# A recommender tower with cross layers: half of the products fused into the sum on VectorE, and one chunk of the first layer split into fp32r passes

## The chip, the cores and the metric

The kernel runs on one core of a Trainium2 chip. The core's engines work side by side, each through its own queue of instructions in order, and wait for one another by semaphores: TensorE (PE) multiplies matrices into PSUM, VectorE (DVE) and ScalarE (ACT) read PSUM and SBUF, GpSimd (POOL) reads SBUF alone, and SyncE (SP) issues DMAs. The metric is the device time of one execution in microseconds (us), lower is better.

## The reference, cut to what matters

512 examples, 32 fields, 32 dimensions. Layer 0 takes products of all pairs of fields and mixes them to 128 maps; layer 1 takes products of the 32 fields with those 128 maps and mixes them again to 128 maps. A small dense tower follows.

```python
e = stack([tbl_f[ids[:, f]] for f in range(32)], axis=1)    # (512, 32, 32)
prev, outs = e, []
for W in (filter_0, filter_1):                              # (32*32, 128), (32*128, 128)
    z = einsum('bhd,bmd->bhmd', e, prev).reshape(b, h * m, d)
    prev = relu(einsum('bpd,pn->bnd', z, W))
    outs.append(prev)
h = concat([sum(concat(outs, axis=1), axis=-1), dense_ctx], axis=1)
y = relu(relu(h @ W_top1 + b_top1) @ W_top2 + b_top2) @ W_top3
```

## The kernel before

The pairs (example, dimension) are the columns. 128 of them make a tile, four tiles a group, and there are 32 groups. The first two groups and the last ones are written out, the ones between run in a hardware loop of three groups a turn (`over_groups`, L97 and on).

**Layer 1, for a tile `u` of a group `g`.** The sum over fields is turned round: for every field h, TensorE multiplies layer 0's output by the field's filter, and the result is scaled by the field's value and then summed over the 32 fields. Four fields fill one PSUM bank (128 columns of a tile on the partitions, 4 x 128 maps along the bank), so a tile has NK = 8 banks, and each bank is made by three matmuls of fp32r operands (high x high, L895; high x low, L896; low x high, L903). Six banks of PSUM are used in a ring: bank k can be written when bank k-6 has been scaled (`layer1`, waits on `act_scaled` and `dve_scaled`). `y_ready` counts finished banks.

**Scaling and summing.** The value of a field is a number per partition (`es`). ScalarE scales banks 0, 1, 3, 5, 6 of each tile, one instruction for each field (L559, 128x128), VectorE the banks 2, 4, 7, one instruction for a bank (L724, 128x512, `es` broadcast). Both write `prod`, which holds all 32 fields of a tile, two fields interleaved word by word (`[F // 2, N, 2]`); the filters of VectorE's banks are stored in that interleaved order (`filters_by_bank`), so it writes without a step, while ScalarE writes every second word. `prod` has three buffers. GpSimd then adds the first 6 fields onto the next 6 (`fold`, L436), and VectorE sums the 26 fields that are left, in two halves of 64 maps each (`reduce`, L737).

**Layer 0, for the next group.** It has KP = 5 chunks of 128 pairs. GpSimd multiplies the pairs of fields of chunk k (L426, `z`), ScalarE rounds them to fp32r (L520, `z_hi`), GpSimd takes the rest (L416, `z_lo`), and TensorE makes three fp32r matmuls of a chunk (L876 to L878), one of the last chunk (L874). `WHOLE = 1` says that chunk 0 is not split: TensorE multiplies it in fp32 (L868). The matmuls of layer 0 for group g+1 stand between the banks of group g, at the places (tile, bank) in `Z_USED_AT`; the tables `Z_AT`, `Z_LO_AT` and `Z_HI_AT` say where GpSimd and ScalarE do theirs. VectorE also takes the rest of layer 0's output (L704), sums it (L710), transposes the fields' values (L679) and sums layer 1's output (L743, L748, L754), once a group each.

The order on each engine is written out by hand in its `body`: a loop over tiles and banks, with the other work hung at given places. On VectorE the halves of a tile's sum stand at bank 6 of the next tile and bank 2 of the one after.

## Time and profile before

| what | value |
|---|---|
| timed runs (three) | 843.12 to 845.85 us, median 843.94 us |
| profiled execution, first to last instruction | 841.7 us |
| TensorE busy | 834.0 us, 99% of the span |
| VectorE busy | 803.9 us, 96% |
| ScalarE busy | 782.8 us, 93% |
| GpSimd busy | 726.7 us, 86% |
| TensorE's granted clock | 1.000 of full speed |

The profiled execution has no time of its own beside the span of its instructions, 841.7 us; the median of the timed runs is 2.2 us above it. Busy time counts each moment once, however many instructions overlap in it. L12 is line 12 of the kernel.

### The profile page before, as it was taken

To read this page: it belongs to the slowest core of one execution; us is meant where nothing else is said; L and a number is where in the kernel's file an instruction comes from. 1 tells how busy PE (TensorE), PEld (TensorE's weight loads), DVE (VectorE), ACT (ScalarE), POOL (GpSimd) and SP (SyncE) were. 2 spreads that over 40 slices of the span, in tenths; PEclk is the share of its full clock that TensorE was granted. 3 is DMA by queue.
4 is the path that set the end of the run, shared out by engine and by line. 5 is a ranking of instruction groups with operands and counts; after the bars stand their busy time and mean duration, and the time that the engine had idled before them with its cause. 6 is when DMAs were issued, how large, how long until landed. Compare 5 with 4: busy or idle time off the path is not lost.

```text
span 841.7 us, 17220 instructions
## 1 busy us (share of the span) xinstructions
PE 834.0 (99%) x3595; PEld 670.1 (80%) x3595; DVE 803.9 (96%) x877; ACT 782.8 (93%) x2779; POOL 726.7 (86%) x550
## 2 busy tenths in 40 slices
PE   8999999999999999999999999999999999999998
PEld 6688888888888888888888888888888888888777
DVE  7699999999999999999999999999999999999996
ACT  4799999999999999999999999999999999999984
POOL 5899888999888899888899888899988799988871
PEclk9999999999999999999999999999999999999999
DMA  5541132332132232122232122332123223212000
GB/s 154 181 134 50 46 85 79 82 85 62 32 84 78 83 84 72 33 73 78 83 84 81 34 62 80 82 83 84 44 50 84 78 84 84 51 44 76 1 13 1
DMA packets 62101, 60.17 MB, mean 71 GB/s; under 512 B 26203, under 2 KB 37083, under 8 KB 62078
## 3 DMA queue, kind: packets, MB, share of 16 engines
q1 hardware_dynamic: 57982, 57.80, 23.3%
q0 software_dynamic: 4096, 2.11, 2.9%
q8 instruction: 9, 0.15, 0.1%
q14 instruction: 14, 0.11, 0.1%
HBM read 55.51 MB, written 4.31 MB: 71 GB/s over the span
## 4 chain that ended last, share of the span: by engine, by line
PE 94%; DVE 2%; DMA 1%; POOL 1%; issue 1%; SPq 0%; ACT 0%; DVEq 0%
PE ps_y L895 27%; PE ps_y L903 27%; PE ps_y L896 27%; PE ps_c L868 3%; PE ps_c L878 3%; PE ps_c L877 2%; PE ps_c L876 2%; POOL gat L447 1%; DVE csum L737 1%; PE ps_c L874 1%; DVE prod L724 1%; DMA prod<-w 0%; DMA gat<-table,rows 0%; DMA ids_and_bounds_sb<-ids_and_bounds 0%; PE ps_y L999 0%
## 5 line engine op out<-in xcount | busy, mean ns | idle before, releaser
L559 ACT ACTIVATE prod<-ps_y,es 128x128 f32<-128x128 f32 x2560 | 719.7, 490 | 37.3 <-PE ps_y L903 34.0
L737 DVE TENSOR_REDUCE csum<-prod 128x64 f32<-128x1664 f32 (+2 forms) x256 | 478.6, 1870 | 0.2
L895 PE MATMUL ps_y<-w_hi,c_both 128*128 128x512 f32 x1024 | 415.4, 406 | 1.8 <-POOL w_lo L454 1.0
L903 PE MATMUL ps_y<-w_hi,c_both 128*128 128x512 f32 x1024 | 399.6, 390 | 0.0
L896 PE MATMUL ps_y<-w_lo,c_both 128*128 128x512 f32 x1024 | 399.5, 390 | 0.0
L724 DVE TENSOR_TENSOR prod<-ps_y,es 128x512 f32<-128x512 f32 x384 | 256.0, 680 | 23.6 <-PE ps_y L903 22.4
L436 POOL TENSOR_TENSOR prod<-prod 128x768 f32<-128x768 f32 (+1 forms) x128 | 240.3, 1878 | 35.9 <-ACT prod L559 28.7
L895 PEld LDWEIGHTS ps_y<-w_hi,c_both 128*128 128x128 f32 x1024 | 192.4, 188 | 54.2 <-issue 10.4
L896 PEld LDWEIGHTS ps_y<-w_lo,c_both 128*128 128x128 f32 x1024 | 192.4, 188 | 48.2 <-issue 8.2
L903 PEld LDWEIGHTS ps_y<-w_hi,c_both 128*128 128x128 f32 x1024 | 192.2, 188 | 42.1
L426 POOL TENSOR_TENSOR z<-first,second 128x512 f32<-128x512 f32 x155 | 198.2, 1295 | 25.0 <-PE ps_c L874 24.9
L416 POOL TENSOR_TENSOR z_lo<-z,z_hi 128x512 fp32r<-128x512 f32 x121 | 154.2, 1293 | 1.3 <-issue 1.3
L407 POOL DMA_INDIRECT gat<-table,rows_now x116 | 111.6, 962 | 28.1 <-issue 21.8
L520 ACT ACTIVATE z_hi<-z 128x512 fp32r<-128x512 f32 x90 | 71.9, 799 | 0.0
L710 DVE TENSOR_REDUCE h<-c_both 128x1024 f32 (+1 forms) x32 | 38.7, 1209 | 0.0
L878 PE MATMUL ps_c<-z_lo,w_hi 128*128 128x512 f32 x90 | 36.6, 407 | 0.0
L877 PE MATMUL ps_c<-z_hi,w_lo 128*128 128x512 f32 x90 | 34.9, 388 | 0.0
L876 PE MATMUL ps_c<-z_hi,w_hi 128*128 128x512 f32 x90 | 34.9, 388 | 0.0
L868 PE MATMUL ps_c<-z,w_sum 128*128 128x512 f32 x68 | 34.7, 591 | 0.0
L520 ACT ACTIVATE z_hi<-z,copy_sb 128x512 fp32r<-128x512 f32 x31 | 27.1, 874 | 0.0
L543 ACT ACTIVATE c_parts<-csum 128x512 f32<-128x512 f32 x31 | 25.2, 812 | 0.0
L704 DVE SCALAR_TENSOR_TENSOR c_both<-ps_c,c_both 128x512 fp32r<-128x512 f32 x31 | 21.2, 683 | 0.0
(119 smaller groups left out, 290.1 us busy)
## 6 DMA issues: line engine op xcount, KB each, us to landing
second<-et_scratch SPq DMA_DIRECT2D x155, 256.0 KB, 3.8
first<-et_scratch SPq DMA_DIRECT2D x31, 256.0 KB, 3.3
et_scratch<-gat SPq DMA_DIRECT2D x62, 64.0 KB
prod<-w SPq DMA_DIRECT2D x4, 512.0 KB, 4.5
h_scratch<-h_sums SPq DMA_DIRECT2D x120, 2.0 KB
gat<-table,rows_now POOLq DMA_INDIRECT x116, 2.4
wt_sb<-wt SPq DMA_DIRECT2D x2, 512.0 KB
rows_now<-rows SPq DMA_DIRECT2D x30, 2.0 KB, 1.8
```

Of the source, the lines that this page charges most:

```text
L407: pool.indirect_dma_start(out=gat[:, g.r, u * D:(u + 1) * D], out_offset=None, in_=table, in_offset=bass.IndirectOffsetOnAxis(ap=rows_now[ ...
L416: nc.gpsimd.tensor_tensor(z_lo[:, k, :], z[:, k, :], z_hi[:, k, :].bitcast(F32), ALU.subtract).then_inc(z_lo_ready, splits_at_once(g))
L426: nc.gpsimd.tensor_tensor(z[:, k, :], first[:, :], second[:, k, :], ALU.mult).then_inc(z_ready, 1)
L436: nc.gpsimd.tensor_tensor(high, high, low, ALU.add).then_inc(folded, 1)
L520: nc.scalar.activation(z_hi[:, k, :], z[:, k, :], ACT.Copy, scale=copy_sb[:, 0:1] if k == LASTK else 1.0).then_inc(z_hi_ready, splits_at_o ...
L559: last = nc.scalar.activation(prod[:, buffer_of(g, u), h // 2, :, h % 2], ps_y[:, bank_of(g, u, k), j * N:(j + 1) * N], ACT.Copy, scale=es ...
L724: nc.vector.tensor_tensor(prod[:, buffer_of(g, u), pairs, :, :], ps_y[:, bank_of(g, u, k), :].rearrange("p (a n t) -> p a n t", n=N, t=2), ...
L737: nc.vector.tensor_reduce(csum[:, g.r, maps, u], prod[:, buffer_of(g, u), fields_folded(g, u) // 2:F // 2, maps, :].rearrange("p a n t -> ...
L878: nc.tensor.matmul(ps_c[:, :], w0_hi[:, k, :], low, start=False, stop=False)
L895: nc.tensor.matmul(out, hi, w_hi, start=True, stop=False)
L896: nc.tensor.matmul(out, hi, w_lo, start=False, stop=False)
L903: nc.tensor.matmul(out, lo, w_hi, start=False, stop=True).then_inc(y_ready, 1)
```

## The change

ScalarE now scales four banks of a tile (0, 2, 4, 6), and VectorE the other four (1, 3, 5, 7). `prod` keeps 16 fields instead of 32: VectorE no longer writes products of its own but adds them onto ScalarE's. For each field of its bank it runs one instruction, `scalar_tensor_tensor`, which multiplies the 128 columns of PSUM by the field's value (read per partition from `es`) and adds the 128 products that ScalarE has left in the partner bank's place, in the same place. So VectorE's bank k waits for ScalarE's bank k-1. GpSimd folds 4 fields onto the next 4, and VectorE's sum runs over the 12 that are left. Chunk 0 of layer 0 is split like the chunks 1 to 3: one more rounding on ScalarE, one more subtraction on GpSimd, and three fp32r matmuls in the place of the one in fp32, at (1, 0) instead of (0, 6). The raw filters get SBUF of their own instead of lying in `prod`, and a wait of ScalarE on the filters in group 0 goes.

```diff
-WHOLE = 1
+WHOLE = 0
-ACT_BANKS = ((0, 1, 3, 5, 6),) * TG
-DVE_BANKS = tuple(tuple(k for k in range(NK) if k not in a) for a in ACT_BANKS)
-FOLD = 6
-FOLD_LAST = (10, 10, 10, 8)
+ACT_BANKS = ((0, 2, 4, 6),) * TG
+PARTNER = {1: 0, 3: 2, 5: 4, 7: 6}
+DVE_BANKS = (tuple(PARTNER),) * TG
+SCALED = HB * len(ACT_BANKS[0])
+FOLD = 4
+FOLD_LAST = (6, 6, 6, 6)
...
-        prod = sb("prod", [P, BUFS, F // 2, N, 2])
+        prod = sb("prod", [P, BUFS, SCALED // 2, N, 2])
+        w1_raw = sb("w1_raw", [P, F, N])
+        w0_raw = sb("w0_raw", [P, 2 * KP, N])
...
+        def place_of(u, k):
+
+            return HB * ACT_BANKS[u].index(k)
...
-            Z_LO_AT = {1: (1, 2), 2: (3, 4)}
+            Z_LO_AT = {0: (0,), 1: (1, 2), 2: (3, 4)}
...
-                    h = HB * k + j
-                    last = nc.scalar.activation(prod[:, buffer_of(g, u), h // 2, :, h % 2],
+                    h, place = HB * k + j, place_of(u, k) + j
+                    last = nc.scalar.activation(prod[:, buffer_of(g, u), place // 2, :, place % 2],
...
-            Z_HI_AT = {(1, 1): (0, 3), (1, 2): (0, 5), (1, 3): (1, 0), (1, 4): (1, 5)}
+            Z_HI_AT = {(1, 0): (0, 1), (1, 1): (0, 3), (1, 2): (0, 5), (1, 3): (1, 0), (1, 4): (1, 5)}
...
-                fields = slice(HB * k, HB * (k + 1))
-                pairs = slice(HB // 2 * k, HB // 2 * (k + 1))
-                nc.vector.tensor_tensor(
-                    prod[:, buffer_of(g, u), pairs, :, :],
-                    ps_y[:, bank_of(g, u, k), :].rearrange("p (a n t) -> p a n t", n=N, t=2),
-                    es[:, g.r, u, fields].rearrange("p (a t) -> p a t", t=2).unsqueeze(2).to_broadcast([P, HB // 2, N, 2]),
-                    ALU.mult).then_inc(dve_scaled, 1)
+                dve.wait_ge(act_scaled, signals(ACT_BANKS, g, u, PARTNER[k]))
+                for j in range(HB):
+                    h, place = HB * k + j, place_of(u, PARTNER[k]) + j
+                    summed = prod[:, buffer_of(g, u), place // 2, :, place % 2]
+                    last = nc.vector.scalar_tensor_tensor(out=summed, in0=ps_y[:, bank_of(g, u, k), j * N:(j + 1) * N],
+                                                          scalar=es[:, g.r, u, h:h + 1], in1=summed,
+                                                          op0=ALU.mult, op1=ALU.add)
+                last.then_inc(dve_scaled, 1)
...
-            Z_USED_AT = ((0, 6), (1, 6), (2, 1), (2, 4), (2, 6))
+            Z_USED_AT = ((1, 0), (1, 6), (2, 1), (2, 4), (2, 6))
```

VectorE's queue, in the loop, from bank 2 of a group's first tile (the second half of a sum, then the next bank, the sum of layer 0's output and a first half). Before:

```order
L724 TENSOR_TENSOR prod<-ps_y,es 128x512 [waits y_ready]
L737 TENSOR_REDUCE csum<-prod 128x64
L721 REGISTER_ALU
L724 TENSOR_TENSOR prod<-ps_y,es 128x512 [waits y_ready]
L710 ISA [waits c_lo_ready]
L710 TENSOR_REDUCE h<-c_both 128x16
L733 ISA
L734 ISA [waits folded]
L735 ISA [waits act_scaled]
L737 TENSOR_REDUCE csum<-prod 128x64 [waits dve_scaled]
```

The same place after the change, from bank 1:

```order
L728 SCALAR_TENSOR_TENSOR prod<-ps_y,es,prod 128x128 [waits act_scaled]
L728 SCALAR_TENSOR_TENSOR prod<-ps_y,es,prod 128x128 x3
L740 TENSOR_REDUCE csum<-prod 128x64
L723 REGISTER_ALU
L724 REGISTER_ALU [waits y_ready]
L728 SCALAR_TENSOR_TENSOR prod<-ps_y,es,prod 128x128 [waits act_scaled]
L728 SCALAR_TENSOR_TENSOR prod<-ps_y,es,prod 128x128 x3
L713 ISA [waits c_lo_ready]
L713 TENSOR_REDUCE h<-c_both 128x16
```

Each bank of VectorE's is now four instructions of 128 columns instead of one of 512, and the first of the four waits for ScalarE as well as for TensorE.

TensorE's queue, in the loop, where chunk 0 of layer 0 stands. Before, behind bank 6 of the first tile:

```order
L903 MATMUL ps_y<-w_hi,c_both 128x512
L867 REGISTER_ALU [waits c_lo_ready]
L868 MATMUL ps_c<-z,w_sum 128x512 [waits z_ready]
L97 REGISTER_ALU
L895 MATMUL ps_y<-w_hi,c_both 128x512 [waits dve_scaled,act_scaled]
```

After, behind bank 0 of the second tile:

```order
L906 MATMUL ps_y<-w_hi,c_both 128x512
L874 REGISTER_ALU [waits c_lo_ready]
L879 MATMUL ps_c<-z_hi,w_hi 128x512 [waits z_lo_ready]
L880 MATMUL ps_c<-z_hi,w_lo 128x512
L881 MATMUL ps_c<-z_lo,w_hi 128x512
L898 MATMUL ps_y<-w_hi,c_both 128x512 [waits dve_scaled,act_scaled]
```

One fp32 matmul has become three of fp32r, and it waits for GpSimd's rest of the chunk (`z_lo`) instead of the product itself.

GpSimd's queue, in the loop, for a group's first tile. Before:

```order
L426 TENSOR_TENSOR z<-first,second 128x512 [waits z_lo_ready]
L97 REGISTER_ALU [waits pairs_in2]
L426 TENSOR_TENSOR z<-first,second 128x512 [waits z_lo_ready]
L97 REGISTER_ALU [waits pairs_in3]
L426 TENSOR_TENSOR z<-first,second 128x512 [waits z_lo_ready]
L432 ISA
L433 ISA [waits act_scaled]
L436 TENSOR_TENSOR prod<-prod 128x768 [waits dve_scaled]
```

After:

```order
L432 TENSOR_TENSOR z<-first,second 128x512 [waits z_lo_ready]
L420 REGISTER_ALU
L99 REGISTER_ALU [waits z_hi_ready]
L422 TENSOR_TENSOR z_lo<-z,z_hi 128x512 [waits l0_done]
L99 REGISTER_ALU [waits pairs_in2]
L432 TENSOR_TENSOR z<-first,second 128x512 [waits z_lo_ready]
L99 REGISTER_ALU [waits pairs_in3]
L432 TENSOR_TENSOR z<-first,second 128x512 [waits z_lo_ready]
L438 ISA
L442 TENSOR_TENSOR prod<-prod 128x512 [waits dve_scaled,act_scaled]
```

The subtraction of chunk 0 has come in behind the first product, and the fold has 512 columns instead of 768.

## Rows read from the trace of the kernel before

**Rows 1.** The page's first part: busy time, share of the span, instructions.

```profile
PE 834.0 (99%) x3595; PEld 670.1 (80%) x3595; DVE 803.9 (96%) x877; ACT 782.8 (93%) x2779; POOL 726.7 (86%) x550
```

**Rows 2.** Windows: stretch, its length, busy time (instructions) by engine, clock, DMA.

```profile
10.00:20.00 10.00, 8.21 (x38) 6.16 (x37) 7.33 (x21) 6.22 (x18) 6.12 (x7) 1.00 0.47 143
...
427.55:452.63 25.08, 25.08 (x110) 20.22 (x109) 24.57 (x27) 24.06 (x88) 22.49 (x18) 1.00 0.28 71
```

**Rows 3.** The chain that ended last, in order of time: start, us, what.

```profile
427.55 0.86 PE ps_c L868 x2
452.63 0.86 PE ps_c L868 x2
```

**Rows 4.** Waits: who waited for whom, total us, times, longest.

```profile
DVE prod L724 <- PE ps_y L903: 22.4, 34, 2.3
...
PE ps_y L895 <- DVE prod L724: 0.8, 1, 0.8
```

**Rows 5.** VectorE by line and shape: count, busy us, mean ns, idle before.

```profile
L737 DVE TENSOR_REDUCE csum<-prod 128x64 f32<-128x1664 f32 x248 | 465.5, 1877 | 0.0
...
L737 DVE TENSOR_REDUCE csum<-prod 128x64 f32<-128x1408 f32 x6 | 9.7, 1611 | 0.0
...
L838 DVE SCALAR_TENSOR_TENSOR z_lo<-ps_c,z_hi 128x480 fp32r<-128x480 f32 x4 | 2.6, 652 | 1.1 <-ACT z_hi L626 1.1
...
L845 DVE TENSOR_SCALAR second<-ps_y,bt_sb 128x480 f32<-128x480 f32 x1 | 0.7, 718 | 1.0 <-PE ps_y L1001 1.0
...
L673 DVE SCALAR_TENSOR_TENSOR w_lo<-w_hi,copy_sb,w_sum 128x128 fp32r<-128x128 f32 x1 | 0.3, 346 | 0.0
...
L698 DVE SCALAR_TENSOR_TENSOR c_both<-ps_h,c_both 128x128 fp32r<-128x128 f32 x1 | 0.3, 291 | 0.1
...
L693 DVE TENSOR_TENSOR z_lo<-z,z_hi 128x128 fp32r<-128x128 f32 x1 | 0.3, 284 | 0.0
```

**Rows 6.** VectorE's timeline in one group: start, us, line, shapes, idle before.

```profile
429.73 1.88 DVE L737 TENSOR_REDUCE csum<-prod 128x64 f32<-128x1664 f32 x1
431.52 1.28 DVE L724 TENSOR_TENSOR prod<-ps_y,es 128x512 f32<-128x512 f32 x2
432.72 1.87 DVE L737 TENSOR_REDUCE csum<-prod 128x64 f32<-128x1664 f32 x1
...
438.09 0.69 DVE L724 TENSOR_TENSOR prod<-ps_y,es 128x512 f32<-128x512 f32 x1 [0.51 <-PE ps_y L903]
```

**Rows 7.** VectorE's timeline in the first 20 us.

```profile
3.56 0.29 DVE L662 TENSOR_SCALAR rows<-neg,ids_and_bounds_sb 128x12 uint32<-128x12 f32 x1
3.76 0.21 DVE L654 CAST idf<-ids_and_bounds_sb 128x116 f32<-128x116 int32 x1
...
7.28 0.69 DVE L670 TENSOR_TENSOR w_lo<-w_sum,w_hi 128x512 fp32r<-128x512 f32 x1
7.89 0.35 DVE L673 SCALAR_TENSOR_TENSOR w_lo<-w_hi,copy_sb,w_sum 128x128 fp32r<-128x128 f32 x1
...
16.57 0.29 DVE L698 SCALAR_TENSOR_TENSOR c_both<-ps_h,c_both 128x128 fp32r<-128x128 f32 x1
16.77 0.54 DVE L684 TENSOR_TENSOR z<-c_parts,ps_y 128x384 f32<-128x384 f32 x1
```

**Rows 8.** ScalarE: L559 alone in one group's window; then L520 by form.

```profile
427.55:452.63 25.08, 22.56 (x82) 1.00 0.28 71
...
L520 ACT ACTIVATE z_hi<-z 128x512 fp32r<-128x512 f32 x90 | 71.9, 799 | 0.0
```

**Rows 9.** GpSimd by line and shape.

```profile
L436 POOL TENSOR_TENSOR prod<-prod 128x768 f32<-128x768 f32 x124 | 229.0, 1847 | 25.3 <-ACT prod L559 23.8
...
L416 POOL TENSOR_TENSOR z_lo<-z,z_hi 128x512 fp32r<-128x512 f32 x121 | 154.2, 1293 | 1.3 <-issue 1.3
```

**Rows 10.** The timeline of all engines near the end.

```profile
830.29 3.42 DVE L737 TENSOR_REDUCE csum<-prod 128x64 f32<-128x1536 f32 x2
...
833.74 0.43 ACT L548 ACTIVATE c_end<-csum 128x128 f32<-128x128 f32 x1 [0.89 <-DVE csum L737]
...
834.33 0.38 PE L1001 MATMUL ps_y<-z_lo,wt_hi 128*128 128x480 f32 x1
```

More of the change, by code:

```diff
@@ L174, in tower @@
         y_sb = sb("y_sb", [1, B])
-        w1_raw, w0_raw = (prod[:, b, :, :, :].rearrange("p a n t -> p (a n t)").rearrange("p (h n) -> p h n", n=N)
-                          for b in (2, 1))
         ids_sb = ids_and_bounds_sb[:, 0:TILES]
@@ L430, in fold @@
                 count = fields_folded(g, u)
-                last_bank = (2 * count - 1) // HB
-                pool.wait_ge(act_scaled, signals(ACT_BANKS, g, u, last_bank))
-                pool.wait_ge(dve_scaled, signals(DVE_BANKS, g, u, last_bank))
+                folded_banks = ACT_BANKS[u][:(2 * count - 1) // HB + 1]
+                pool.wait_ge(act_scaled, signals(ACT_BANKS, g, u, folded_banks[-1]))
+                pool.wait_ge(dve_scaled, signals(DVE_BANKS, g, u, max(k for k in DVE_BANKS[u] if PARTNER[k] in folded_banks)))
                 buf = buffer_of(g, u)
@@ L592, in body @@
                     for k in range(NK):
-                        if number == 0 and (u, k) == (2, 0):
-                            act.wait_ge(w1_lo_ready, NK - 2)
-                            act.wait_ge(w1_last_lo, 2)
                         if number == 0 and (u, k) == (0, 3):
@@ L719, in scale @@
                         dve.wait_ge(es_ready, g.times(1, 1))
-                    wait(dve, reduced, g.times(TG * HALVES, (u + 1 - BUFS) * HALVES))
                 dve.wait_ge(y_ready, g.times(TG * NK, u * NK + k + 1))
-                fields = slice(HB * k, HB * (k + 1))
-                pairs = slice(HB // 2 * k, HB // 2 * (k + 1))
-                nc.vector.tensor_tensor(
-                    prod[:, buffer_of(g, u), pairs, :, :],
-                    ps_y[:, bank_of(g, u, k), :].rearrange("p (a n t) -> p a n t", n=N, t=2),
-                    es[:, g.r, u, fields].rearrange("p (a t) -> p a t", t=2).unsqueeze(2).to_broadcast([P, HB // 2, N, 2]),
-                    ALU.mult).then_inc(dve_scaled, 1)
+                dve.wait_ge(act_scaled, signals(ACT_BANKS, g, u, PARTNER[k]))
[6 more added lines that the diff above has]
+                last.then_inc(dve_scaled, 1)
             def reduce(g, u, half):
@@ L736, in reduce @@
                 maps = slice(half * N // HALVES, (half + 1) * N // HALVES)
-                nc.vector.tensor_reduce(csum[:, g.r, maps, u], prod[:, buffer_of(g, u), fields_folded(g, u) // 2:F // 2, maps, :].rearrange("p a n t -> p n a t"),
+                nc.vector.tensor_reduce(csum[:, g.r, maps, u], prod[:, buffer_of(g, u), fields_folded(g, u) // 2:SCALED // 2, maps, :].rearrange("p a n t -> p n a t"),
                                         AX.XY, ALU.add).then_inc(reduced, 1)
@@ L1052, in filters_by_bank @@
 def filters_by_bank(w1):
-    w = w1.reshape(NK, HB, N, N).transpose(2, 0, 1, 3)
-    out = np.empty((N, NK, HB * N), w1.dtype)
-    for k in range(NK):
-        bank = w[:, k]
-        if k in DVE_BANKS[0]:
-            bank = bank.reshape(N, HB // 2, 2, N).transpose(0, 1, 3, 2)
-        out[:, k] = bank.reshape(N, HB * N)
-    return out.reshape(N, F, N)
+    return np.ascontiguousarray(w1.reshape(F, N, N).transpose(1, 0, 2))
 def row_picks():
```

## The prediction

> **What bounds the kernel now.** I read the page's busy times first. TensorE is busy in 99% of the span, but VectorE stands at 96% and ScalarE at 93% [rows 1], so no engine has much room, and what the change does to VectorE matters as much as what it does to TensorE. The chain of work that ended last runs through TensorE and passes the same place, layer 0's chunk 0 in fp32, once a group: from 427.55 to 452.63 us, a period of 25.08 us [rows 3]. In the window of just that group TensorE is busy 25.08 of 25.08 us, VectorE 24.57, ScalarE 24.06, GpSimd 22.49 [rows 2]. The list of waits says the same from the other side: VectorE waited 22.4 us in all for TensorE's banks, TensorE once for VectorE, 0.8 us [rows 4], and in VectorE's timeline of the group there is one gap, 0.51 us, ended by TensorE [rows 6]. So TensorE sets the period, and VectorE follows at a distance of 0.51 us in 25.08, or 2%.
>
> **VectorE's work in a group, taken apart.** Mean durations overlap, so I count from start to start. A sum over 1664 columns begins at 429.73 and the next instruction at 431.52: 1.79 us. The two products that follow begin at 431.52 and the sum after them at 432.72: 0.60 us each [rows 6]. A group has 8 half sums and 12 products: 8 x 1.79 + 12 x 0.60 = 14.32 + 7.20 = 21.52 us. The rest of the 24.57, 3.05 us, are the once-a-group instructions (L679, L704, L710, L743, L748, L754), which the change leaves as they are.
>
> **The sums get shorter.** They run over 12 fields instead of 26, 768 columns instead of 1664. From 1408 to 1664 columns the duration grows from 1611 to 1877 ns [rows 5], 1.04 ns a column, so 896 columns less are 0.93 us less: 1.79 - 0.93 = 0.86 us, 6.88 us for eight. VectorE gains 7.44 us a group.
>
> **The products get longer; this is the disputed cost.** 12 instructions of 512 columns become 64 of 128 columns, which read PSUM and SBUF, take their scalar from SBUF per partition, and write where they read. No row before has all of this. The nearest row is L698, a scalar_tensor_tensor of 128x128 out of PSUM and SBUF with a constant as its scalar: 291 ns [rows 5], and the next instruction begins 0.20 us after it, at 16.77 after 16.57 [rows 7]. That is the lower end.
>
> What does the scalar from SBUF add? L673, the same shape from SBUF with such a scalar, takes 346 ns, against 284 for L693, the same shape without one; L845 with one takes 718 ns at 480 columns out of PSUM, L838 without one 652 [rows 5]. So 62 to 66 ns in the duration. Is it also in the spacing? Two places say yes. L662, 12 columns with two such scalars, begins at 3.56 and the next at 3.76, 0.20 us for a dozen columns. And L673 began 0.61 us after L670, the usual spacing of 512 columns, and still took its full 0.35 us, so nothing of the scalar's load had been done while L670 ran [rows 7]. I take 0.20 + 0.062, rounded to 0.265 us, as that start to start is read to a hundredth. The upper end without a new effect is 0.28, half a hundredth for each reading and the larger of the two increments. 64 x 0.265 = 16.96 us, against 7.20 before.
>
> **VectorE's new group:** 6.88 + 16.96 + 3.05 = 26.89 us, over today's period. The waits that come in cost nothing beside it: VectorE's bank k waits for ScalarE's bank k-1, and ScalarE becomes the lighter engine. Once VectorE is the slowest, TensorE fills the ring of six banks ahead of it and ScalarE finishes its own banks early.
>
> **The other engines.** ScalarE has 64 instead of 80 products, each 22.56 / 80 = 0.28 us of a group [rows 8], so 4.5 us less, and one rounding more, at most 0.80 us [rows 8]: about 20.4 us. GpSimd's four folds go from 1.85 us to what 512 columns cost, 1.29 [rows 9], 2.2 us less, and one subtraction of 1.29 comes in: about 21.6 us. The fold waits for VectorE's bank 3 and must be done by VectorE's bank 5 of the next tile, some five banks later at 1.06 us each plus two sums, 7.0 us; before the longest stretch of its own GpSimd has three products and the new subtraction, 4 x 1.29 = 5.2 us, and the fold makes 6.5. It fits. TensorE: the fp32 chunk took 0.86 us [rows 3]; the other 106 matmuls of the group share 25.08 - 0.86 = 24.22, or 0.2285 us each, so three in fp32r take 0.69 and the group 24.90 us. That gain of 0.18 us a group is real, but it now ends in a wait for VectorE. TensorE's clock should not fall for having gaps: in the stretch from 10 to 20 us TensorE was busy 8.21 of 10 us at a granted clock of 1.00, the level of 2.4 GHz [rows 2].
>
> A rule of the Trainium skill (VectorE: DVE Perf Modes, The TRN2 errata) gives a VectorE instruction out of PSUM 120 cycles of 0.96 GHz beside its columns: 258 ns for 128, before the scalar. By that the estimate would be 0.32 us, 20.5 us for 64, and some 160 us more on the run. L698's spacing of 0.20 us [rows 7] speaks against it, and the sum goes by the row.
>
> **The sum.** From group 1's start to the last group's start there are 30 periods. Each goes from 25.08 to 26.89 us, +1.81, together +54 us. For the two ends I take nothing: in group 0 VectorE waits for TensorE and can take more work, and at the end VectorE's last sum (830.29 + 3.42 = 833.7, then ScalarE's 0.43 to 834.17) was no later than TensorE's own last products, which began until 834.33 [rows 10], so shorter sums win nothing there. Span 841.7 + 54 = 896 us; the timed median stood 2.2 us over the profiled span, so **898 us**.
>
> **The rivals.**
>
> *A, the scalar's load is hidden.* If VectorE fetches the next instruction's scalar while it reads PSUM, leaving one of its paths to SBUF free, the spacing is 0.20 us: 12.8 + 6.88 + 3.05 = 22.7 us, below TensorE's 24.90. Then TensorE stays the bound and the split pays: 30 groups by 0.18 us, -5 us, 839 us. This is the side opposite to my forecast, and it decides at a spacing of (24.90 - 9.93) / 64 = 0.234 us. For it speaks that neither of my two places has an instruction out of PSUM behind another one; against it, both places and L845.
>
> *C, the step of two words costs.* VectorE's old products wrote four fields without a step, and the sums read pairs of words. The new instruction reads and writes every second word of `prod`, and no row of VectorE's does that. If a word alone costs as much as a pair, 128 columns stream like 256: another 128 x 1.04 = 0.13 us, spacing 0.40, 25.5 + 9.93 = 35.4 us a group, +10.3 us by 30, **1154 us**. Against it: ScalarE writes exactly these places today, 0.28 us for 128 columns, without a visible penalty, though it is another engine. The Trainium skill (Vector Engine (DVE) Microarchitecture Reference, Measured stream behaviour on trn2) has this as a rule: full rate only for runs of two neighbouring words, and 1.73 to 1.98 ns a column where every element hops; an estimate from its figures is 0.35 to 0.39 us an instruction. The Trainium skill (SBUF — State Buffer, Door 1: The DMA port swizzle, the note on cachelines) says otherwise, that two hits in a line of 16 bytes suffice, which a step of 8 bytes gives. No run here shows which holds.
>
> *D, the waits come first.* VectorE's wait for ScalarE could leave gaps though no engine is full: where ScalarE does two pieces of layer 0 and a bank in a row (0.80 + 1.1 us) behind a bank, VectorE's partner bank comes late. Under a full VectorE such a gap is covered by its own backlog; at a spacing below 0.234 it lies beside TensorE's ring, 6 banks by 0.69 us, or 4.1 us. A small loss on rival A, giving about 844 us: no change.
>
> **How the numbers follow.** My forecast, VectorE the bound by the scalar's cost, spacing 0.245 to 0.28: 0.57. A: 0.20. C: 0.18. D and what lies between: 0.05. A measurement of this kernel can tell about 0.3% (2.5 us) from no change. Faster takes A without its neighbours, 0.20; same 0.03; slower 0.77. Within my forecast, the spacing's end of 0.28 gives 17.92 + 9.93 = 27.85 us, +83 us, 927 us; the lower end, 0.245, 25.61, +16, 860 us. A range from 860 to 927 would hold only 0.57, so it reaches to A and takes that in: 835 to 930, holding 0.80 with D; C is left out.
>
> **What would show it.** In the changed profile: the mean of L740 near 944 ns (0.86 start to start); the spacing of L728, 0.265 where I am right, 0.20 under A, 0.35 or more under C; the period between two of TensorE's chunk 0, 26.9 us; VectorE with no gap in a group, TensorE's waits at L898 ended by VectorE's L728; three matmuls of L879 to L881 taking 0.69 us. The prediction is wrong if L728's spacing is under 0.234, or if GpSimd's fold ends VectorE's waits.

## The result and the profile after

| what | before | after |
|---|---|---|
| timed runs (four each), median | 844.05 us (843.12 to 845.85) | 885.48 us (885.35 to 885.73) |
| ratio of after to before | | 1.0492, 95% interval 1.0479 to 1.0505 |
| profiled execution, first to last instruction | 841.7 us | 883.7 us |

The change makes the kernel 4.9% slower. The forecast was 898 us; 885 lies 13 us below it and inside its range.

The page of the changed kernel, busy time by engine, which answers to [rows 1]:

```profile
PE 860.6 (97%) x3625; PEld 667.9 (76%) x3625; DVE 861.5 (97%) x2541; ACT 702.2 (79%) x2297; POOL 693.3 (78%) x580
```

VectorE has 57.6 us of busy time more. ScalarE and GpSimd, relieved by the change, now stand still for a fifth of the span, and the longest wait of the kernel is ScalarE's. The list of waits (who, for whom; us in total, times, longest), beside [rows 4]:

```profile
ACT prod L565 <- PE ps_y L906: 138.6, 238, 2.6
POOL prod L442 <- DVE prod L728: 55.3, 36, 10.0
POOL prod L442 <- ACT prod L565: 50.9, 30, 1.9
...
PE ps_y L898 <- DVE prod L728: 10.9, 38, 0.5
```

TensorE waited for VectorE once before and does so 38 times now. That VectorE is the cause, and not merely full too, is seen in its own timeline of one group (start, us, line, shapes, idle time before where there is any), beside [rows 6]:

```profile
449.13 1.23 DVE L713 TENSOR_REDUCE h<-c_both 128x1024 f32 x1
...
452.15 2.17 DVE L728 SCALAR_TENSOR_TENSOR prod<-ps_y,es,prod 128x128 f32<-128x128 f32 x8
454.22 0.97 DVE L740 TENSOR_REDUCE csum<-prod 128x64 f32<-128x768 f32 x1
455.08 2.18 DVE L728 SCALAR_TENSOR_TENSOR prod<-ps_y,es,prod 128x128 f32<-128x128 f32 x8
...
472.78 1.13 DVE L728 SCALAR_TENSOR_TENSOR prod<-ps_y,es,prod 128x128 f32<-128x128 f32 x4 [0.16 <-issue]
...
475.72 1.21 DVE L713 TENSOR_REDUCE h<-c_both 128x1024 f32 x1
```

Read it from start to start. Eight fused products begin at 452.15 and the sum behind them at 454.22: 2.07 / 8 = 0.258 us each. The sum begins at 454.22 and the next product at 455.08: 0.86 us. The only idle time that the timeline lists in 26.59 us is 0.16 us, and no engine ended it. The window of that group, in the columns of [rows 2], says the same:

```profile
449.13:475.72 26.59, 26.15 (x112) 20.37 (x111) 26.43 (x79) 20.96 (x70) 20.93 (x19) 1.00 0.25 69
```

VectorE is busy 26.43 of 26.59 us. (TensorE's 26.15 includes matmuls that last longer in the trace where TensorE waits: the L898 at 453.44, which waited for VectorE, has 0.47 us, the others 0.39.) The mean durations by line and shape, beside [rows 5], and what ended the idle time before them:

```profile
L728 DVE SCALAR_TENSOR_TENSOR prod<-ps_y,es,prod 128x128 f32<-128x128 f32 x2048 | 570.5, 365 | 7.8 <-PE ps_y L906 5.1 <-ACT prod L565 1.9 <-issue 0.4
L740 DVE TENSOR_REDUCE csum<-prod 128x64 f32<-128x768 f32 x248 | 240.3, 969 | 0.0
```

Of VectorE's waits before 2048 fused products, those for ScalarE make 1.9 us in the whole run: the dependence that the change brings in costs next to nothing here.

### The profile page after: what moved, and what is told of

Same layout as the page of the kernel before. It is cut to its first block, busy times and chain, and to the rows that moved or that the text cites. A ratio compares the mean times of both kernels' runs of the same rounds, so it can differ in the third digit from the quotient of the medians.

```text
span 883.7 us, 18757 instructions
## 1 busy us (share of the span) xinstructions
PE 860.6 (97%) x3625; PEld 667.9 (76%) x3625; DVE 861.5 (97%) x2541; ACT 702.2 (79%) x2297; POOL 693.3 (78%) x580
## 4 chain that ended last, share of the span: by engine, by line
PE 56%; DVE 26%; issue 9%; ACT 3%; POOL 3%; DMA 1%; DVEq 1%; SPq 0%; ACTq 0%; POOLq 0%
DVE prod L728 18%; PE ps_y L906 16%; PE ps_y L898 16%; PE ps_y L899 15%; DVE csum L740 4%; ACT prod L565 3%; DVE h L713 2%; PE ps_c L881 2%; PE ps_c L879 2%; PE ps_c L880 2%; DVE c_both L707 2%; POOL z L432 1%; POOL gat L453 1%; PE ps_c L877 1%; DMA w_raw<-w 0%
## 5 line engine op out<-in xcount | busy, mean ns | idle before, releaser
L565 ACT ACTIVATE prod<-ps_y,es 128x128 f32<-128x128 f32 x2048 | 589.5, 389 | 153.8 <-PE ps_y L906 138.6
L728 DVE SCALAR_TENSOR_TENSOR prod<-ps_y,es,prod 128x128 f32<-128x128 f32 x2048 | 570.5, 365 | 7.8 <-PE ps_y L906 5.1
L898 PE MATMUL ps_y<-w_hi,c_both 128*128 128x512 f32 x1024 | 411.2, 402 | 12.8 <-DVE prod L728 10.9
L442 POOL TENSOR_TENSOR prod<-prod 128x512 f32<-128x512 f32 (+1 forms) x128 | 168.0, 1312 | 123.7 <-DVE prod L728 55.3
L898 PEld LDWEIGHTS ps_y<-w_hi,c_both 128*128 128x128 f32 x1024 | 192.3, 188 | 87.1 <-issue 25.8
L740 DVE TENSOR_REDUCE csum<-prod 128x64 f32<-128x768 f32 (+1 forms) x256 | 246.8, 964 | 0.3 <-POOL prod L442 0.3
L422 POOL TENSOR_TENSOR z_lo<-z,z_hi 128x512 fp32r<-128x512 f32 x151 | 193.4, 1299 | 18.2 <-ACT z_hi L526 17.8
L413 POOL DMA_INDIRECT gat<-table,rows_now x116 | 111.9, 965 | 26.8 <-issue 20.4
L881 PE MATMUL ps_c<-z_lo,w_hi 128*128 128x512 f32 x120 | 48.8, 407 | 0.0
L880 PE MATMUL ps_c<-z_hi,w_lo 128*128 128x512 f32 x120 | 46.8, 390 | 0.0
L713 DVE TENSOR_REDUCE h<-c_both 128x1024 f32 (+1 forms) x32 | 39.3, 1228 | 0.0
L879 PEld LDWEIGHTS ps_c<-z_hi,w_hi 128*128 128x128 f32 x120 | 22.5, 188 | 5.3 <-POOL z_lo L422 0.6
L880 PEld LDWEIGHTS ps_c<-z_hi,w_lo 128*128 128x128 f32 x120 | 22.5, 188 | 4.8
L881 PEld LDWEIGHTS ps_c<-z_lo,w_hi 128*128 128x128 f32 x120 | 22.4, 187 | 4.7
```

The costliest lines, as they stand in the source:

```text
L413: pool.indirect_dma_start(out=gat[:, g.r, u * D:(u + 1) * D], out_offset=None, in_=table, in_offset=bass.IndirectOffsetOnAxis(ap=rows_now[ ...
L422: nc.gpsimd.tensor_tensor(z_lo[:, k, :], z[:, k, :], z_hi[:, k, :].bitcast(F32), ALU.subtract).then_inc(z_lo_ready, splits_at_once(g))
L442: nc.gpsimd.tensor_tensor(high, high, low, ALU.add).then_inc(folded, 1)
L565: last = nc.scalar.activation(prod[:, buffer_of(g, u), place // 2, :, place % 2], ps_y[:, bank_of(g, u, k), j * N:(j + 1) * N], ACT.Copy, ...
L728: last = nc.vector.scalar_tensor_tensor(out=summed, in0=ps_y[:, bank_of(g, u, k), j * N:(j + 1) * N], scalar=es[:, g.r, u, h:h + 1], in1=s ...
L740: nc.vector.tensor_reduce(csum[:, g.r, maps, u], prod[:, buffer_of(g, u), fields_folded(g, u) // 2:SCALED // 2, maps, :].rearrange("p a n ...
```

## The experiments

They come in three questions: what a fused product costs and why; what the split is worth; and whether another division of the banks saves the idea. Unless it says otherwise, a kernel is the changed one with one edit.

### What the fused product pays for

**const_scalar.** The scalar is a constant instead of a number per partition.

```diff
-                                                          scalar=es[:, g.r, u, h:h + 1], in1=summed,
+                                                          scalar=1.0, in1=summed,
```

> The changed kernel, with the constant 1.0 as the scalar of VectorE's 64 fused products; it leaves out the scaling by the field's value in VectorE's banks. Theory (VectorE sets the period, and the scalar read from SBUF is about 0.06 us of each product's 0.258): spacing 0.20 us, VectorE's group 12.8 + 6.9 + 3.05 = 22.7 us, TensorE becomes the bound again at about 24.9 us a group, 838 to 842 us. Rival (the excess over the bare columns comes from the step of two words or from writing where one reads, not from the scalar): spacing stays at 0.25 or more, 880 to 886 us.

Measured: 847.06 us, ratio to before 1.0033 (1.0021 to 1.0046). VectorE's timeline:

```profile
431.41 1.69 DVE L728 SCALAR_TENSOR_TENSOR prod<-ps_y,prod 128x128 f32<-128x128 f32 x8
432.99 0.97 DVE L740 TENSOR_REDUCE csum<-prod 128x64 f32<-128x768 f32 x1
...
453.07 0.89 DVE L728 SCALAR_TENSOR_TENSOR prod<-ps_y,prod 128x128 f32<-128x128 f32 x4 [1.94 <-PE ps_y L906]
```

Eight products in 1.58 us, 0.20 each: the spacing of L698 in [rows 7], in place of 0.258. So the scalar from SBUF costs 0.06 us an instruction. Taking it out gives back 38 us of the 41 us lost, because VectorE's group falls from 26.4 to about 22.7 us, below TensorE's. The run did not come down to the 838 to 842 us of TensorE's bound, though: with VectorE relieved, gaps appear at the turn of the loop, such as the 1.94 us above. The profile puts this one down to TensorE, but TensorE had finished that bank at 450.29 us, 2.78 us before (banks counted from the first of the run). These gaps are read below, with rival A and in the last section.

**no_step.** The fused products read and write neighbouring words of `prod` (the maps land in other places).

```diff
-                    summed = prod[:, buffer_of(g, u), place // 2, :, place % 2]
+                    summed = prod[:, buffer_of(g, u), place // 2, (place % 2) * N // 2:(place % 2 + 1) * N // 2, :].rearrange("p n t -> p (n t)")
```

> The changed kernel, with VectorE's fused products reading and writing 128 neighbouring words of the same pair of fields instead of every second word; it sums the maps in wrong places, with the same instructions, sizes and waits. Theory (a step of two words costs nothing on VectorE): spacing 0.258 as in the changed kernel, 883 to 888 us. Rival (the step has a share of the 0.258): each 0.01 us of it gives back 64 x 0.01 x 30 = 19 us, down to 840 us where it is 0.024 or more.

**step_four.** The other direction: they touch every fourth word.

```diff
-                    summed = prod[:, buffer_of(g, u), place // 2, :, place % 2]
+                    summed = prod[:, buffer_of(g, u), place // HB * 2:place // HB * 2 + 2, :, :].rearrange("p a n t -> p (a n t)").rearrange("p (n s) -> p n s", s=HB)[:, :, j]
```

> The changed kernel, with VectorE's fused products reading and writing every fourth word of the bank's 512 words instead of every second word of a pair of fields; it sums the maps in wrong places. One theory (what counts is whether two elements in a row lie in one line of 16 bytes, which a step of two words still gives and a step of four does not): 0.10 to 0.13 us more an instruction, spacing 0.36 to 0.39, 64 x 0.10 to 0.13 = 6.4 to 8.3 us a group more, 1080 to 1135 us. The other (any constant step streams at one column a cycle): 0.258, 883 to 888 us.

Measured: no_step 885.6 us, ratio to before 1.0485 (1.0466 to 1.0503); step_four 1066.27 us, 1.2622 (1.2599 to 1.2644). VectorE's timeline without a step:

```profile
452.44 2.19 DVE L728 SCALAR_TENSOR_TENSOR prod<-ps_y,es,prod 128x128 f32<-128x128 f32 x8
454.51 0.98 DVE L740 TENSOR_REDUCE csum<-prod 128x64 f32<-128x768 f32 x1
```

and with a step of four:

```profile
504.44 3.01 DVE L728 SCALAR_TENSOR_TENSOR prod<-ps_y,es,prod 128x128 f32<-128x128 f32 x8
507.26 1.04 DVE L740 TENSOR_REDUCE csum<-prod 128x64 f32<-128x768 f32 x1
```

No step and a step of two words have the same spacing, 2.07 / 8 = 0.258 us. A step of four takes 2.82 / 8 = 0.352 us, 0.094 us more, a little under the 0.10 to 0.13 expected; 64 of them by 30 groups are 180 us, and that is the run's difference to after, 180.8 us.

### What the split is worth

**whole_chunk.** The split is taken back: chunk 0 in fp32, at its old place.

```diff
-WHOLE = 0
+WHOLE = 1
...
-            Z_LO_AT = {0: (0,), 1: (1, 2), 2: (3, 4)}
+            Z_LO_AT = {1: (1, 2), 2: (3, 4)}
...
-            Z_USED_AT = ((1, 0), (1, 6), (2, 1), (2, 4), (2, 6))
+            Z_USED_AT = ((0, 6), (1, 6), (2, 1), (2, 4), (2, 6))
```

> The changed kernel, with chunk 0 of layer 0 in fp32 again, at its old place, and its rounding and subtraction gone. Theory (VectorE sets the period, TensorE's 0.18 us a group end in a wait for VectorE): no change, 883 to 888 us, ratio to the changed kernel within 0.3%. Rival (TensorE and VectorE bound in turn, since TensorE is still busy 97% of the span): 30 x 0.18 = 5 us more, 890 us.

Measured: 885.36 us, ratio to before 1.049 (1.0469 to 1.0511), the time of the full change. Beside VectorE's 26.4 us a group the split neither wins nor costs.

**split_only.** The kernel before with the split alone.

```diff
-WHOLE = 1
+WHOLE = 0
...
-            Z_LO_AT = {1: (1, 2), 2: (3, 4)}
+            Z_LO_AT = {0: (0,), 1: (1, 2), 2: (3, 4)}
...
-            Z_HI_AT = {(1, 1): (0, 3), (1, 2): (0, 5), (1, 3): (1, 0), (1, 4): (1, 5)}
+            Z_HI_AT = {(1, 0): (0, 1), (1, 1): (0, 3), (1, 2): (0, 5), (1, 3): (1, 0), (1, 4): (1, 5)}
...
-            Z_USED_AT = ((0, 6), (1, 6), (2, 1), (2, 4), (2, 6))
+            Z_USED_AT = ((1, 0), (1, 6), (2, 1), (2, 4), (2, 6))
```

> The kernel before with chunk 0 of layer 0 split, and nothing else of the change. Theory (the split gives TensorE 0.18 us a group, and TensorE is the bound there): 30 x 0.18 = 5 us less, 838 to 840 us. Rival (the rounding and the subtraction that come in make ScalarE, 24.06 + 0.6 us a group, or GpSimd, 22.5 + 1.3, or what waits for them the bound): 842 to 850 us.

Measured: 886.0 us, ratio 1.0493 (1.0479 to 1.0508). Neither expectation holds: the split alone, meant to save TensorE 0.18 us a group, loses as much as the whole change. VectorE's fused products have no part in this. The waits of that kernel show who has:

```profile
DVE prod L724 <- PE ps_y L903: 62.4, 43, 2.3
POOL z_lo L416 <- ACT z_hi L520: 52.1, 30, 2.7
PEld ps_c L876 <- POOL z_lo L416: 47.3, 38, 1.9
...
PE ps_c L876 <- POOL z_lo L416: 31.0, 38, 1.5
```

VectorE waits for TensorE, TensorE for GpSimd's `z_lo`, and GpSimd for ScalarE's rounding of chunk 0, as its timeline shows:

```profile
448.40 1.30 POOL L416 TENSOR_TENSOR z_lo<-z,z_hi 128x512 fp32r<-128x512 f32 x1 [1.42 <-ACT z_hi L520]
...
471.85 1.30 POOL L426 TENSOR_TENSOR z<-first,second 128x512 f32<-128x512 f32 x1
475.75 1.29 POOL L416 TENSOR_TENSOR z_lo<-z,z_hi 128x512 fp32r<-128x512 f32 x1 [2.60 <-ACT z_hi L520]
477.00 2.54 POOL L426 TENSOR_TENSOR z<-first,second 128x512 f32<-128x512 f32 x2
```

The split has put a subtraction at the start of GpSimd's group that needs a rounding which ScalarE does in that same group, behind bank 1. GpSimd's next two products and its fold stand behind it in the queue. The wait is 1.4 to 1.5 us in two groups of three and 2.6 in the third, at the turn of the loop (52.1 us in 30 times). In the group from 422.24 to 448.40 GpSimd is busy for 23.80 us; with this wait and 0.9 us of other gaps that makes its 26.16 us, against 25.08 before. 30 times 1.08 us are 32 of the 42 us lost; the other 10 or so lie in the groups at the turn, 27.3 us each.

**split_early** puts that reading to the test: split_only with the rounding a group's end earlier, and GpSimd's subtraction ahead of the product in each step.

```diff
-                        if n < len(products) and (number is None or number + products[n][0] < GROUPS):
-                            multiply(g.plus(products[n][0]), products[n][1])
                         if n < len(splits):
                             split_z(g.plus(1), splits[n])
+                        if n < len(products) and (number is None or number + products[n][0] < GROUPS):
+                            multiply(g.plus(products[n][0]), products[n][1])
...
-            Z_HI_AT = {(1, 0): (0, 1), (1, 1): (0, 3), (1, 2): (0, 5), (1, 3): (1, 0), (1, 4): (1, 5)}
+            Z_HI_AT = {(2, 0): (3, 7), (1, 1): (0, 3), (1, 2): (0, 5), (1, 3): (1, 0), (1, 4): (1, 5)}
```

> The kernel before with the first chunk split, as in split_only (886.0 us), but ScalarE rounds chunk 0 of the next group one group's end earlier (behind bank 7 of tile 3, step (3,7), in place of (0,1)), and GpSimd takes the subtraction ahead of the product in each of its steps. Theory: split_only lost its time because GpSimd stood 2.6 us a group at the head of its queue for that rounding, with 23.8 us of work beside it. With the rounding done before, that wait goes, GpSimd's group is 23.8 us, under TensorE's 24.90, and the time comes back to 838 to 843 us. Rival: GpSimd's and ScalarE's added work (1.3 and 0.7 us a group) binds by itself, in whatever order: 860 to 886 us, with GpSimd or ScalarE without gaps in a group.

Measured: 844.57 us, ratio 0.9999 (0.999 to 1.0008). The same work in another order gives the 41 us back, so the wait was the cause and GpSimd's added work was not. (Which of the two moves did it, the earlier rounding or the subtraction ahead of the product, the run doesn't tell.) What does not come is the gain of 5 us. Three groups of this kernel in windows, with the columns of [rows 2]:

```profile
454.74:479.62 24.88, 24.88 (x111) 20.36 (x109) 24.35 (x27) 24.88 (x91) 23.33 (x19) 1.00 0.31 72
479.62:504.68 25.06, 25.06 (x110) 20.40 (x109) 24.56 (x27) 24.79 (x90) 24.00 (x19) 1.00 0.25 71
504.68:530.02 25.34, 25.34 (x111) 20.31 (x110) 24.84 (x27) 23.86 (x85) 24.04 (x19) 1.00 0.26 71
```

The first has the 24.88 us that the split should give; the mean of the three is 25.09, against 25.08 before. VectorE, with about 24.5 us of work, and ScalarE stand so close behind TensorE that what it wins in one group it loses waiting in the next, for a bank to be scaled. From 454 to 530 us the list of its weight loads' waits is:

```profile
PEld ps_y L895 <- DVE prod L724: 0.7, 2, 0.3
PEld ps_y L895 <- ACT prod L559: 0.5, 2, 0.4
```

### Another cost of the same instruction, and other divisions

**bank_const.** VectorE's four fused products of a bank become one addition of 512 columns, without scaling.

```diff
-                for j in range(HB):
-                    h, place = HB * k + j, place_of(u, PARTNER[k]) + j
...
-                                                          op0=ALU.mult, op1=ALU.add)
+                pairs = slice(place_of(u, PARTNER[k]) // 2, place_of(u, PARTNER[k]) // 2 + HB // 2)
+                summed = prod[:, buffer_of(g, u), pairs, :, :].rearrange("p a n t -> p a t n")
+                last = nc.vector.tensor_tensor(summed, ps_y[:, bank_of(g, u, k), :].rearrange("p (a t n) -> p a t n", t=2, n=N),
+                                               summed, ALU.add)
```

> The changed kernel, with one addition of a bank's 512 columns onto ScalarE's products in the place of four fused products; it leaves out the scaling by the field's value in VectorE's banks, like const_scalar, but VectorE's loop has 12 instructions a tile fewer. const_scalar came to 847.06 us, some 8 us over TensorE's own work, with a gap at the turn of the loop (every third group, 75.6 us instead of 74.7) and 97 packets of instructions fetched instead of 14. Theory (VectorE's longer loop is fetched anew at every turn, and that is the 8 us): packets near 14 again, every group 24.9 us, 837 to 841 us. Rival (the 8 us come from VectorE's wait for ScalarE's partner bank, 52 us in all in const_scalar): the same waits and 845 to 849 us.

Measured: 845.4 us, ratio 1.0016 (1.0007 to 1.0026). The theory's 837 to 841 us and 14 packets did not come (the page counts 54); the time lies in the rival's range. VectorE is busy for 676.5 us only (80%), and it waits longer for ScalarE's banks, 121.9 us in 199 times against 52.2 in 87 in const_scalar. In the list of waits the third place is the one that split_only had:

```profile
POOL z_lo L422 <- ACT z_hi L526: 45.7, 29, 2.8
```

So GpSimd's head of queue is in the changed kernel too. But neither wait is what holds this kernel up. The starts of L713, once a group, at the turn of the loop:

```profile
403.08 1.21 DVE L713 TENSOR_REDUCE h<-c_both 128x1024 f32 x1
427.92 1.21 DVE L713 TENSOR_REDUCE h<-c_both 128x1024 f32 x1
454.35 1.21 DVE L713 TENSOR_REDUCE h<-c_both 128x1024 f32 x1
```

An ordinary group takes 24.84 us, though GpSimd waits 1.18 us for the rounding in it: with folds of 512 columns instead of 768 it has room for that (busy 21.6 us in an ordinary group of const_scalar, 23.8 in one of split_only). What is lost is lost in the group at the turn, 26.43 us here, and the last section reads it.

**fold_six.** GpSimd folds 6 fields instead of 4, so that VectorE sums 640 columns.

```diff
-FOLD = 4
+FOLD = 6
```

> The changed kernel with 6 fields folded by GpSimd instead of 4. Theory (VectorE sets the period and nothing else does): eight half sums of 640 columns instead of 768, 0.133 us less each, 1.06 us a group, 30 groups: 32 us less, 852 to 856 us. Rival (GpSimd's longer fold, 1.85 us instead of 1.29, comes late for VectorE's sum): 865 us or more, with VectorE's sum waiting for GpSimd's fold.

**five_three.** With 6 fields folded, ScalarE takes five banks and VectorE three in every second tile.

```diff
-ACT_BANKS = ((0, 2, 4, 6),) * TG
-PARTNER = {1: 0, 3: 2, 5: 4, 7: 6}
+ACT_BANKS = ((0, 2, 4, 6), (0, 2, 4, 5, 6)) * (TG // 2)
+PARTNERS = ({1: 0, 3: 2, 5: 4, 7: 6}, {1: 0, 3: 2, 7: 6}) * (TG // 2)
...
-FOLD = 4
+FOLD = 6
```

> The changed kernel with 6 fields folded, and in every second tile five banks for ScalarE and three for VectorE. VectorE's group: 56 fused products at 0.258, four half sums of 640 and four of 896 columns, 14.45 + 2.91 + 3.97 + 3.05 = 24.4 us, under TensorE's 24.9. Theory: TensorE becomes the bound again and the split pays, 838 to 848 us, the upper end if the turn of the loop costs as in const_scalar. Rival (with all four engines near 24 us the waits between them cost): 850 to 860 us.

Measured: fold_six 906.35 us, ratio 1.0735 (1.0719 to 1.0752); five_three 914.56 us, 1.0837 (1.0822 to 1.0852). Both were to be faster than the change, and both are slower, though VectorE has less to do. The waits of fold_six:

```profile
POOL prod L442 <- DVE prod L728: 93.9, 45, 10.0
ACT z_hi L526 <- POOL z L432: 46.8, 53, 3.4
...
DVE prod L728 <- ACT prod L565: 34.6, 69, 1.8
PE ps_c L879 <- POOL z_lo L422: 29.5, 29, 2.1
```

No engine is full; as these totals read, they wait round in a circle: GpSimd's fold for VectorE, ScalarE's rounding for GpSimd's product behind that fold, TensorE for `z_lo`, VectorE for ScalarE. GpSimd's timeline shows the fold at the head:

```profile
474.61 1.85 POOL L442 TENSOR_TENSOR prod<-prod 128x768 f32<-128x768 f32 x1 [2.00 <-DVE prod L728]
```

**fold_six_early** and **five_three_early** take the early rounding of split_early into both, the subtraction first, and the fold of tile 2 behind the next product.

```diff
+                    if u == 3 and (number is None or number + 1 < GROUPS):
+                        fold(g, 2)
...
-                    fold(g, u)
+                    if u != 2 or (number is not None and number + 1 >= GROUPS):
+                        fold(g, u)
```

> The changed kernel with 6 fields folded (as fold_six, 906.35 us), the same early rounding, the subtraction first, and GpSimd's fold of tile 2 put behind the product of the next step. Theory: fold_six was lost in a ring of waits (GpSimd's fold at the head of its queue for VectorE, its subtraction behind it, TensorE for that, VectorE for TensorE), not in work; without it VectorE's shorter sums set the period: 8 sums of 640 columns, 0.73 us each by 1.04 ns a column off 0.86, so 5.84 + 16.5 + 3.05 = 25.4 us, 852 to 858 us. Rival: the wait is in the longer fold itself (1.85 us for 768 columns) or returns at another tile: 885 to 906 us.

> As five_three (914.56 us: in every second tile ScalarE takes five banks and VectorE three, 6 fields folded), with the same early rounding, subtraction first and the late fold of tile 2. Theory: the order of GpSimd's queue was the loss; then VectorE has some 23 to 24 us a group, TensorE is the bound again with 24.90 us, and the time is 838 to 848 us. Rival: waits between ScalarE's and VectorE's banks or GpSimd's fold keep a ring: 860 us and more.

Measured: fold_six_early 893.34 us, ratio 1.0576 (1.056 to 1.0592); five_three_early 869.98 us, 1.0299 (1.0284 to 1.0315). The edit gives back 13 us of fold_six and 45 us of five_three, but the rivals' numbers came true: GpSimd's fold still waits for VectorE, 79.9 us in 91 times and 47.2 us in 64, and in fold_six_early ScalarE's rounding waits more than before for GpSimd's product, 88.7 us instead of 46.8. Nor are the 45 us of five_three all won by the order: its ordinary groups take 26.6 us, a turn of three groups 82.4, while five_three_early has even groups of 25.8. About half of the 45 us is the longer turn, some 2.5 us nine times, which went with the same edit.

**own_fold.** VectorE's sums go to places that GpSimd does not fold, so that the fold needs ScalarE alone; VectorE has 13 banks of a group instead of 16 (14 in five_three_early, against which the diff is). The fold of tile 2 is back at its place, and four of ScalarE's roundings stand one or two banks later.

```diff
-ACT_BANKS = ((0, 2, 4, 6), (0, 2, 4, 5, 6)) * (TG // 2)
-PARTNERS = ({1: 0, 3: 2, 5: 4, 7: 6}, {1: 0, 3: 2, 7: 6}) * (TG // 2)
+ACT_BANKS = ((0, 1, 3, 5, 6), (0, 1, 3, 6), (0, 1, 3, 5, 6), (0, 1, 3, 5, 6))
+PLACES = ((1, 3, 5, 0, 6), (1, 3, 0, 6), (1, 3, 5, 0, 6), (1, 3, 5, 0, 6))
+PARTNERS = ({2: 0, 4: 0, 7: 6}, {2: 0, 4: 0, 5: 0, 7: 6}, {2: 0, 4: 0, 7: 6}, {2: 0, 4: 0, 7: 6})
...
-FOLD = 6
+FOLD = (6, 4, 6, 6)
...
-                pool.wait_ge(dve_scaled, signals(DVE_BANKS, g, u, max(k for k in DVE_BANKS[u] if PARTNERS[u][k] in folded_banks)))
```

> The fused products in another division: ScalarE takes five banks of a tile and VectorE three (in tile 1 four and four), VectorE adds its banks onto places that GpSimd does not fold (banks 0 and 6), so that the fold waits for ScalarE alone; 6 fields folded (tile 1: 4); chunk 0 split, rounded early as in split_early, the other roundings two banks later. Theory: what five_three_early and fold_six_early lost over their work was the ring through GpSimd's fold of VectorE's sums; without it each engine's work decides. VectorE: 13 banks of 4 products by 0.258 us, 13.4, and sums of 896 columns, 6 by 0.99 us, and of 768, 2 by 0.86 us, 7.7, with 3.05 us of the rest 24.1 us; ScalarE a bank less than in split_early, about 23.2; GpSimd about 23.3; TensorE 24.9 and the bound: 838 to 843 us. Rival: the waits return in another place (VectorE's bank for ScalarE's, ScalarE's rounding for GpSimd's product), as in five_three_early: 850 to 870 us.

Measured: 848.66 us, ratio 1.0048 (1.0035 to 1.0062): between the two expectations, 6 us over the theory's and just under the rival's. It is the best of the kernels with fused products that compute everything. Its waits:

```profile
POOL prod L442 <- ACT prod L565: 52.2, 35, 7.3
...
PEld ps_c L882 <- POOL z_lo L423: 15.2, 30, 1.3
```

and GpSimd's timeline at the fold of tile 2:

```profile
468.78 1.86 POOL L442 TENSOR_TENSOR prod<-prod 128x768 f32<-128x768 f32 x1 [1.07 <-ACT prod L565]
```

The circle through VectorE is gone. A smaller wait is left: GpSimd's fold of tile 2 stands 1.07 us at the head of the queue for ScalarE's bank, and TensorE about 0.5 us a group for `z_lo`, 15.2 us in 30 times. As own_fold changes the division, the partners and the roundings together, it doesn't say how much each of them gave. None of the kernels beats the one before.

## Why the prediction was right

The range of 835 to 930 us was wide enough to hold rival A as well, so that the time lies in it says little. What the runs bear out is the direction and the mechanism, step by step.

**The bound moves from TensorE to VectorE: right.** VectorE is busy without a gap of its own making in the group, and TensorE waits for its banks. Of the sign list, "TensorE's waits at L898 ended by L728" is true of the rows for PE, 10.9 us; the weight loads' waits are put down to ScalarE and to "issue" as well, so that sign was less clear than written. The three matmuls of chunk 0 took the 0.69 us forecast (449.28 to 449.97).

**The sums, 0.86 us: right** (454.22 to 455.08). Their mean duration, forecast at 944 ns, is 969; start to start it makes no difference.

**The scalar's cost, taken at 0.062 us: the mechanism right, the size a little high.** This is the term that was mis-sized: the spacing is 0.258 us and not 0.265, 64 x 0.258 = 16.5 instead of 16.96 us a group. With it the group is 16.5 + 6.88 + 3.05 = 26.4 us, and the mean over seven groups in VectorE's timeline is the same (L713, once a group, at its first and last start):

```profile
396.52 1.21 DVE L713 TENSOR_REDUCE h<-c_both 128x1024 f32 x1
...
581.25 1.23 DVE L713 TENSOR_REDUCE h<-c_both 128x1024 f32 x1
```

184.73 / 7 = 26.39 us, 0.50 less than forecast, by 30 groups 15 us; the two ends, taken at nothing, gave 2 to 3 us back. Two readings to a hundredth of a microsecond and a sum rounded up from 0.262: 64 a group made that visible. const_scalar shows that the difference to L698's 0.20 us is the scalar. It also lets the growth of VectorE's products, 9.3 us a group, be taken apart: four banks more at the old 0.60 us are 2.4, four instructions at 0.20 us in the place of one of 0.60 are 3.2 in 16 banks, and the scalar makes 3.7.

**A rule that spoke of more, and did not hold.** The trace gives 0.20 us for 128 columns out of PSUM with a constant scalar, 0.258 with one from SBUF. The Trainium skill (VectorE: DVE Perf Modes, The TRN2 errata) would have 258 ns before the scalar; const_scalar's rows, 200 ns, disagree. The 258 ns measured with the scalar are not the rule's 258: without the scalar they fall to 200.

**Rival A, the load is hidden: refuted,** as to mechanism by the spacing, and also as to its time. Had the spacing been 0.20 us, the kernel would have run 847 us and not 839: const_scalar is that case. The window of an ordinary group of it has what rival A reckoned with, TensorE at 24.85 us, but the group with the loop's turn takes more than the difference back (the same columns, three groups of const_scalar):

```profile
403.79:428.64 24.85, 24.85 (x110) 20.48 (x110) 23.05 (x80) 21.40 (x73) 21.56 (x19) 1.00 0.27 72
428.64:455.52 26.88, 26.47 (x116) 21.52 (x116) 23.11 (x80) 21.79 (x73) 22.06 (x20) 1.00 0.25 68
455.52:479.42 23.90, 23.86 (x104) 19.15 (x104) 22.90 (x79) 20.83 (x71) 21.04 (x19) 1.00 0.28 75
```

The second window holds 116 matmuls and the third 104, against 110, so only the sum of the three is to be read. The mean is 25.21 us, more than the 25.08 of before. So the chance on "faster" stood on a case that did not come out faster with this kernel's loop.

**Rival C, a step of two words: refuted by no_step.** A step of two words costs nothing, a step of four 0.094 us in 128 columns. Of the two rules that the prediction set against each other, the runs side with the Trainium skill's note on lines of 16 bytes (SBUF — State Buffer, Door 1: The DMA port swizzle, the note on cachelines), in which a step of 8 bytes still finds two words of a line and one of 16 bytes doesn't; the rule of runs of two neighbouring words (Vector Engine (DVE) Microarchitecture Reference, Measured stream behaviour on trn2) would have put the cost at a step of two already. That a line is the cause is the reading that fits, not something these runs show by themselves.

**The split, "real, but ends in a wait for VectorE": right, for a reason the prediction had only half.** whole_chunk shows it hidden. The prediction costed GpSimd and ScalarE by the sum of their work (21.6 and 20.4 us; the window has 20.93 and 20.96) and said "it fits". It fits behind VectorE, and with the changed kernel's shorter folds it fits beside TensorE too (bank_const's 24.84 us). With the folds of before it doesn't: split_only loses 42 us, most of it on a head of queue that no sum of work shows, and split_early gets them back by order alone. The prediction looked at what is queued behind the fold, and not at what is queued behind the new subtraction.

## What to carry to other kernels

Fusing a multiplication into the sum shortens the sum behind it, but here it turned one broad instruction into four narrow ones, and each pays its fixed part and the load of its scalar: VectorE's products grew from 7.2 to 16.5 us a group, and the shorter sums gave back 7.4. When work is added to an engine that is not full, look first at which wait its new instruction carries and at what stands behind it in the queue: the same subtraction and rounding cost 42 us or nothing, by their places. An estimate by busy time gives the best case: each edit that was to win by moving load (fold_six, five_three, own_fold) lost to waits first. And a wait in the list costs something only where the period shows it: GpSimd's 45.7 us in bank_const left the ordinary groups at TensorE's pace.

## What the runs showed of the hardware beside that

The loop's turns cost time in some kernels. The page counts the packets that fetched instructions; before, and after:

```profile
q14 instruction: 14, 0.11, 0.1%
```

```profile
q14 instruction: 97, 0.79, 0.3%
```

In the changed kernel two groups of a turn take 26.30 us and the third 26.6 (L713 at 422.82, 449.13 and 475.72); before, the periods are even, 25.08 and 25.07. In const_scalar, with 97 packets too, three groups take 75.63 us against 3 x 24.85, some 1.1 us lost a turn, which over nine turns is about the 8 us that it stays above TensorE's bound. bank_const, with 54 packets, loses as much a turn. own_fold and five_three_early, with 17 and 18 packets, have even groups again, 25.18 us and 25.8 us, although their programs have a little more instructions than the change.

What stands still at the turn is ScalarE first. In const_scalar, TensorE's last matmul for the first bank of a turn, and ScalarE's bank before it and that first bank:

```profile
449.22 0.39 PE L906 MATMUL ps_y<-w_hi,c_both 128*128 128x512 f32 x1
```

```profile
448.29 1.15 ACT L565 ACTIVATE prod<-ps_y,es 128x128 f32<-128x128 f32 x4 [0.21 <-PE ps_y L906]
451.16 1.15 ACT L565 ACTIVATE prod<-ps_y,es 128x128 f32<-128x128 f32 x4 [1.73 <-PE ps_y L906]
```

The bank is finished at 449.61 us, and the sums that must have left its place in `prod` ended at 447.1; ScalarE begins 1.56 us after the bank. (The profile names TensorE, which was long done.) Over the nine turns ScalarE begins its first bank 1.37 us on average after TensorE has finished it, in the other groups 0.04 us; in bank_const 1.36 and 0.04; before the change 0.06 everywhere. Five of the 97 packets fall between 449 and 455 us. GpSimd's wait for the rounding grows at the turn as well (in bank_const from 1.18 to 2.77 us), but it begins behind ScalarE's gap, at 450.06 us against 449.21 there, and what it waits for stands behind that gap in ScalarE's queue.

Many packets alone do not make a turn long: step_four, with 97, has even groups (32.1 to 32.2 us), where ScalarE waits some 2 us for its first bank in every group, and split_early, with 54, has 25.05 to 25.2 us. So ScalarE standing for its instructions is the reading that fits where it has no such wait; whose instructions the packets bring, and why two programs of nearly the same length differ, the page doesn't tell, and no run changes that alone.
